# Last half's norms moved from GpSimd to VectorE, with new orders for the last pieces of a four-stage kernel

## What is computed

```python
# attention layer (six of them), per batch of 1024 rows
h1 = _ln(h + sa, l1w, l1b)
h2 = _ln(h1, l2w, l2b)
ff = relu(h2 @ w1.T + b1) @ w2.T + b2
h  = _ln(h2 + ff, l3w, l3b)
# seam
x = x + h                      # then
x = x + _L1_ffn_ref(_layernorm(x))
# last block: every linear quantizes its input in blocks of 16
xq = fp4_quant_dequant(x)
h  = silu(xq @ wq_gate.T) * (xq @ wq_up.T)
y  = fp4_quant_dequant(h) @ wq_down.T
```

## Time and profile before

| what | value |
| --- | --- |
| median of 3 runs | 2740.74 us (2735.45 to 2745.2) |
| profiled execution, its own time | 2755.81 us |
| its span, first to last instruction | 2754.0 us |
| busy share TensorE / VectorE / ScalarE / GpSimd | 86% / 88% / 83% / 57% |
| mean granted TensorE clock | 0.948 of full speed |
| the last two row maxima of the attention | start 2619.03 us into the span |

### The profile page before, as it was taken

The page is one execution under the profiler, slowest core; times in us unless marked ns, Lnnn a source line. Parts: engine busy times, 40 slices in busy tenths (PEclk is TensorE's granted clock), DMA queues, the critical chain, the costliest instruction groups (busy, mean ns, idle before and its releaser), DMA issues.

```text
span 2754.0 us, 93639 instructions
## 1 busy us (share of the span) xinstructions
PE 2356.9 (86%) x38225; PEld 1248.3 (45%) x38225; DVE 2422.1 (88%) x3331; ACT 2297.2 (83%) x4208; POOL 1562.0 (57%) x2959
## 2 busy tenths in 40 slices
PE   5777576799999998999989998999999999899846
PEld 3444365344444444444444444444444444444435
DVE  4888744799999999999999999999999999999956
ACT  5888533599999999999999999999999999999832
POOL 4879764535664466544664456644665446643564
PEclk8888888799999999999999999999999999999977
DMA  3222223311101111011110111101010111100000
GB/s 95 78 92 73 69 77 84 90 48 51 45 29 39 49 47 43 25 48 42 54 36 32 48 35 57 35 37 48 31 54 31 48 43 37 35 33 11 2 1 16
DMA packets 52140, 127.22 MB, mean 46 GB/s; under 512 B 6017, under 2 KB 40705, under 8 KB 47233
## 3 DMA queue, kind: packets, MB, share of 16 engines
q1 hardware_dynamic: 43329, 113.12, 12.3%
q0 software_dynamic: 2432, 5.08, 0.6%
q10 hardware_dynamic: 5952, 3.04, 0.4%
HBM read 96.09 MB, written 29.18 MB: 45 GB/s over the span
## 4 chain that ended last, share of the span: by engine, by line
PE 35%; issue 19%; POOL 17%; DVE 12%; ACT 12%; DMA 1%; POOLq 0%; SPq 0%; ACTq 0%; DVEq 0%; another core or an unknown queue 0%
PE bank L708 11%; PE bank L777 11%; PE bank L788 9%; ACT E L1048 9%; DVE NM L1417 8%; POOL hC L1553 2%; POOL acc L1659 2%; POOL H L1669 1%; ACT acc L999 1%; POOL smp L1652 1%; POOL H L1672 1%; PE bank L689 1%; POOL hC L1556 1%; POOL dg L1717 1%; PE bank L702 1%
## 5 line engine op out<-in xcount | busy, mean ns | idle before, releaser
L1417 DVE TENSOR_REDUCE NM<-bank 128x1 f32<-128x1024 f32 x1536 | 1799.6, 1208 | 73.2 <-PE bank L777 52.5
L1048 ACT ACTIVATE E<-bank,NM 128x1024 f32<-128x1024 f32 x1536 | 1707.4, 1118 | 161.6 <-DVE NM L1417 135.8
L777 PE MATMUL bank<-KS,QS 72*32 72x512 bf16 x12288 | 957.3, 387 | 161.9 <-ACT E L1048 112.4
L788 PE MATMUL bank<-E,dg 128*32 128x256 f32 x12288 | 924.6, 385 | 1.7 <-ACT acc L999 1.7
L1717 POOL TENSOR_TENSOR dg<-mask,RZ 128x128 f32<-128x128 f32 x384 | 152.9, 398 | 823.9 <-DVE RZ L1427 728.1
L777 PEld LDWEIGHTS bank<-KS,QS 72*32 72x32 bf16 x12288 | 251.8, 96 | 706.9 <-ACT E L1048 592.6
L788 PEld LDWEIGHTS bank<-E,dg 128*32 128x32 f32 x12288 | 384.7, 111 | 290.2 <-issue 60.9
L1048 ACT ACTIVATION_READ_ACCUMULATOR E<-bank,NM 128x1 f32 x1536 | 310.7, 202 | 0.0
L1659 POOL TENSOR_TENSOR acc<-acc,rel 128x256 f32<-128x256 f32 x384 | 272.2, 729 | 7.8 <-ACT acc L999 7.8
L708 PE MATMUL bank<-H,ET 128*32 128x129 f32 x6144 | 189.3, 275 | 6.3 <-DVE ET L1360 6.3
L708 PE MATMUL bank<-hT,WL 128*32 128x256 f32 x2304 | 164.0, 388 | 26.3 <-ACT UB L1010 22.0
(11 more groups left out here) (261 smaller groups left out, 2679.4 us busy)
## 6 DMA issues: line engine op xcount, KB each, us to landing
QS<-scratch SPq DMA_DIRECT2D x69, 384.0 KB
KS<-scratch SPq DMA_DIRECT2D x22, 1152.0 KB
scratch<-UB SPq DMA_DIRECT2D x144, 128.0 KB
CB<-crows SPq DMA_DIRECT2D x32, 512.0 KB, 3.8
WL<-in_wl SPq DMA_DIRECT2D x6, 1091.0 KB, 21.4
KS<-scratch SPq DMA_DIRECT2D x6, 384.0 KB
first<-in_fill SPq DMA_DIRECT2D x8, 247.5 KB, 4.2
second<-in_fill SPq DMA_DIRECT2D x8, 247.5 KB, 4.1
```

Of the source, the lines that this page charges most:

```text
L777: inst = PE_.matmul(bank[x % 3][32 * i:32 * i + 32, k * 512:k * 512 + 512], QS[0:72, half % 2, 4 * hq + i, r0:r0 + 32], KS[0:72, b, k, 4 * ...
L788: inst = PE_.matmul(pb(6)[32 * k:32 * k + 32, 256 * grp:256 * grp + 256], dg[:, x // 4 % 3, x % 4, :], E[:, x % NE, :].rearrange("p (i k c ...
L1048: A_.activation(E[:, x % NE, :], bank[x % 3][:, :], ACT.Exp, bias=NM[:, x % 4:x % 4 + 1], accum_out=ZS[:, quad % 3, j:j + 1]).then_inc(s[" ...
L1417: V.tensor_reduce(NM[:, x % 4:x % 4 + 1], bank[x % 3][:, :], AX.X, ALU.max, negate=True).then_inc(s["rowmax"], 1)
```

## The change

The last half's three norms no longer use `pv` and `ln`. On VectorE `nv` aggregates the statistics (`bn_aggr`, one a tile) and adds epsilon; GpSimd's `pw` is now a single power; `na` computes (x - mean) * gain and `nb` that times the power plus the offset, each one combined instruction a row tile, four a norm. For the third norm `nb` adds into `X`, so `fin` goes as a piece of its own, and GpSimd adds the offset to `X` beforehand (`xb`). The second norm's result goes to the `H` buffer. `h2t` may start tile by tile. `END_DUE` and `LAST` have new orders, and a table `NEAR_DUE` for half 22 puts its third norm later. No work of the attention steps is touched.

```diff
-            "POOL": {(7, "f"): "pv0", (8, "f"): "pw0", (9, "f"): "ln00 ln01 ln02 ln03 ln04 ln05 ln06",
...
+           "DVE": {(7, "e"): "nv0 na0 nb0", (8, "m"): "bn10 bn11 bn12 bn13 nv1 na1 nb1",
+                (11, "m"): "add2 bn20 bn21 bn22 bn23 nv2 na2", (12, "m"): "nb2"},
+           "POOL": {(7, "f"): "pw0", (8, "f"): "pw1", (11, "d"): "hb0 hb1", (11, "f"): "xb", (13, "f"): "pw2"}}
...
+        def end_norm_dve(e, own, n, p):
+            a, k = n % 2, int(p[2])
+            var = smp[:, a, k, :, :]
+            src, dst = (ZA[:, a], ZA[:, a], HB)[k], (ZA[:, a], next_h(n), HB)[k]
+            gain, offset = (wl(n // 4, "ln", 256 * k + 128 * i, 128) for i in range(2))
+            if p[:2] == "nv":
+                if k == 0:
+                    e.wait_ge(s["tbn0"], 4 * n + 4)
+                    own.count(V.scalar_tensor_tensor(var[:, :, 3], ZW[:, a, :, 128], EPS / 4.0, ZW[:, a, :, 128], ALU.mult, ALU.mult))
+                else:
+                    e.wait_ge(s["tbn"], 8 * n + 5 * k - 1)
+                for t in range(4):
+                    own.count(V.bn_aggr(var[:, t, 0:2], st[:, a, k, t, :]))
+                e.wait_ge(own.sem, own.n)
+                if k == 0:
+                    V.tensor_tensor(var[:, :, 2], var[:, :, 1], var[:, :, 3], ALU.add).then_inc(s["tbn0"], 1)
+                else:
+                    V.tensor_scalar(var[:, :, 2], var[:, :, 1], EPS, None, ALU.add).then_inc(s["tbn"], 1)
+            elif p[:2] == "na":
+                for t in range(4):
+                    own.count(V.scalar_tensor_tensor(dst[:, t, :], src[:, t, :], var[:, t, 0:1], gain, ALU.subtract, ALU.mult))
+            else:
+                e.wait_ge(own.sem, own.n)
+                e.wait_ge(s["tpow"], 3 * n + k + 1)
+                for t in range(4):
+                    r = n // 2 % 2 * 8 + 4 * (n % 2) + t
+                    out, more = (X[:, r, :], X[:, r, :]) if k == 2 else (dst[:, t, :], offset)
+                    inst = V.scalar_tensor_tensor(out, dst[:, t, :], var[:, t, 3:4], more, ALU.mult, ALU.add)
...
+            elif p[:2] == "pw" and n == HALF_N - 1:
...
+                G.tensor_tensor(smp[:, a, k, :, 3], smp[:, a, k, :, 2], mhalf[:, 0:4], ALU.pow).then_inc(s["tpow"], 1)
+            elif p == "xb":
+                r0 = b * 8 + 4 * hf
+                G.tensor_tensor(X[:, r0:r0 + 4, :], X[:, r0:r0 + 4, :],
+                                wl(l, "ln", 640, 128).unsqueeze(1).to_broadcast([128, 4, 128]), ALU.add)
```

More of the change, by code:

```diff
@@ L179 @@
                 (46, "d"): "sp08 sp09", (46, "f"): "sp10 sp11 sp12 sp13", (47, "d"): "sp14 sp15"}}
-END_DUE = {"PE": {(17, "h"): "h2t", (18, "h"): "ff1_00 ff1_01", (19, "g"): "ff1_10 ff1_11",
[14 rows of a table removed]
-STEPS = PAIRS + 71
-LAST = {"PE": {(1, "g"): "wt", (10, "g"): "tq0", (13, "g"): "gu0", (16, "g"): "gu1", (18, "h"): "tq1", (19, "h"): "ht0",
[5 rows of a table removed]
+NEAR_DUE = {engine: dict(at) for engine, at in HALF_DUE.items()}
+NEAR_DUE["DVE"] = {(11, "m"): "bn10 bn11", (11, "e"): "bn12 bn13", (29, "e"): "add2", (38, "m"): "bn20 bn21 bn22 bn23"}
+NEAR_DUE["POOL"] = {at: HALF_DUE["POOL"][at] for at in HALF_DUE["POOL"] if at[0] < 35}
+NEAR_DUE["POOL"].update({(37, "f"): "pv2", (38, "d"): "pw2", (38, "f"): "ln20 ln21 ln22 ln23", (42, "d"): "ln24 ln25 ln26 ln27 fin"})
+END_DUE = {"PE": {(8, "g"): "h2t", (8, "h"): "ff1_00 ff1_01", (9, "h"): "ff1_10 ff1_11",
[6 rows of a table added]
+STEPS = PAIRS + 71
+LAST = {"PE": {(3, "g"): "wt", (6, "g"): "tq0", (7, "g"): "gu0", (8, "g"): "tq1", (9, "g"): "gu1", (12, "g"): "ht0 gu2", (13, "g"): "dn0 ht1 dn1",
[3 rows of a table added]
         "DVE": {(-14, "m"): "wq00", (-14, "e"): "wq01", (-13, "m"): "wq02", (-13, "e"): "wq03", (-12, "m"): "wq04",
@@ L254, in due @@
     for half in range(max(-2, step // 32 - 3), min(HALF_N, step // 32 + 1)):
-        places = END_DUE if half == HALF_N - 1 else HALF_DUE
+        places = END_DUE if half == HALF_N - 1 else NEAR_DUE if half == HALF_N - 2 else HALF_DUE
         for p in places[engine].get((step - 32 * half - 31 - (8 if half == -2 else 0), place), "").split():
@@ L728, in post_pe @@
             elif p == "h2t":
-                e.wait_ge(s["tln"], 12 * n + 8)
+                src = HB[:, :, :] if n < HALF_N - 1 else next_h(n)
+                if n < HALF_N - 1:
+                    e.wait_ge(s["tln"], 12 * n + 8)
                 for t in range(4):
-                    inst = PE_.transpose(o[:, t * 128:t * 128 + 128], HB[:, t, :], ident[:, :])
+                    if n == HALF_N - 1:
+                        e.wait_ge(s["add1"], TILES + t + 1)
+                    inst = PE_.transpose(o[:, t * 128:t * 128 + 128], src[:, t, :], ident[:, :])
                 inst.then_inc(s["h2t"], 1)
@@ L1185, in scan_dve @@
                 for n, x in PROJECT["DVE"].get(p, ()):
-                    post_dve(e, n, x)
+                    post_dve(e, own, n, x)
                 if p in KNOWN["DVE"]:
@@ L1345, in unit_dve, with post_dve @@
                     V.scalar_tensor_tensor(x[:, 0:128], pb(n % 2)[:, 0:128], 0.5, x[:, 0:128], ALU.mult, ALU.add).then_inc(s["unit_out"], 1)
-        def post_dve(e, n, p):
+        def end_norm_dve(e, own, n, p):
[26 more added lines that the diff above has]
+                    inst = V.scalar_tensor_tensor(out, dst[:, t, :], var[:, t, 3:4], more, ALU.mult, ALU.add)
+                    if k == 0:
+                        own.count(inst)
+                    elif k == 1:
+                        inst.then_inc(s["add1"], 1)
+                    elif t == 3:
+                        inst.then_inc(s["fin"], 1)
+        def post_dve(e, own, n, p):
+            if p[:2] in ("nv", "na", "nb"):
+                end_norm_dve(e, own, n, p)
+                return
             if p in ("part1", "part3"):
@@ L1378, in post_dve @@
                 if k == 1:
-                    e.wait_ge(s["tln"], 12 * n + 1 + t)
+                    if n < HALF_N - 1:
+                        e.wait_ge(s["tln"], 12 * n + 1 + t)
+                    else:
+                        e.wait_ge(own.sem, own.n)
                 elif t == 0:
@@ L1428, in attention_dve @@
                 for n, p in due("DVE", q, "m"):
-                    post_dve(e, n, p)
+                    post_dve(e, own, n, p)
                 for j, p in second("DVE", q, "m"):
@@ L1647, in post_pool @@
                     G.tensor_tensor(y[:, :, 0], y[:, :, 0], y[:, :, 3], ALU.add).then_inc(s["tvar"], 1)
+            elif p[:2] == "pw" and n == HALF_N - 1:
+                k = int(p[2])
+                if k == 0:
+                    e.wait_ge(s["tbn0"], 4 * n + 5)
+                else:
+                    e.wait_ge(s["tbn"], 8 * n + 5 * k)
+                G.tensor_tensor(smp[:, a, k, :, 3], smp[:, a, k, :, 2], mhalf[:, 0:4], ALU.pow).then_inc(s["tpow"], 1)
[3 more added lines that the diff above has]
+                                wl(l, "ln", 640, 128).unsqueeze(1).to_broadcast([128, 4, 128]), ALU.add)
             elif p[:2] == "pw":
@@ L1677, in post_pool @@
                 h = int(p[2])
-                e.wait_ge(s["tln"], 12 * n + 6 + 2 * h)
-                G.tensor_tensor(ZA[:, a, 2 * h:2 * h + 2, :], HB[:, 2 * h:2 * h + 2, :],
+                if n < HALF_N - 1:
+                    e.wait_ge(s["tln"], 12 * n + 6 + 2 * h)
+                else:
+                    e.wait_ge(s["add1"], TILES + 2 + 2 * h)
+                h2 = HB[:, :, :] if n < HALF_N - 1 else next_h(n)
+                G.tensor_tensor(ZA[:, a, 2 * h:2 * h + 2, :], h2[:, 2 * h:2 * h + 2, :],
                                 wl(l, "ln", 768, 128).unsqueeze(1).to_broadcast([128, 2, 128]), ALU.add).then_inc(s["h2b"], 2)
```

## The result

| | before | changed |
| --- | --- | --- |
| median, first measurement (4 runs each) | 2740.20 us | 2722.95 us (2722.21 to 2733.77) |
| ratio | 1 | 0.9947, 95% interval 0.9932 to 0.9961 |
| median, second measurement (21 and 6 runs) | 2738.44 us | 2726.85 us (2722.72 to 2731.10) |
| ratio | 1 | 0.9960, 95% interval 0.9948 to 0.9973 |
| span of the profiled execution | 2754.0 us | 2731.9 us |

The kernel is faster: 14.5 us by the first ratio, 11.0 by the second. The forecast was 2722, range 2711 to 2733, 19 us less. The time lies within the range, but the gain is smaller than forecast, and one has to look at the parts to see by how much.

A forecast was written before the change was run, and what follows sets the result against it. The attention is bound by its own queues and unchanged; the tail is VectorE's work and waits. Start 2630.7 + work 86.3 + waits 8.2 + end 9.85 = 2735.1 against 2754.0, 19 us less: 2722 us, range 2711 to 2733.

The forecast's parts named there:

- The start: Start of VectorE's own tail: half 22's third norm moved behind the last `rel`, so `turn` starts 3.5 us earlier, at 2630.0.
- VectorE's work: VectorE's busy time in the tail: 78.7 us before, 89.3 with the norms, less 3.0 for less GpSimd interference, 86.3.
- VectorE's waits: VectorE's idle time in the tail: 27.0 us before, 8.2 after (2.6 before `sw0`, 5.6 in the loop).
- To the second norm's result: Last half's path to the second norm's result: 2643.7 against 2664.16, the largest step, 20 us earlier.
- The sum of the feed-forward: Start of `add2` in the last half: at 2664 us against 2692.31 before.
- the rival of the feed-forward's chain: `h2t` to `add2` takes 28 us again instead of 20, so the end comes later: 2733 us, chance 0.12.
- The end: Requantization, transposes, down projection and store behind `qh7`: 9.85 us, left alone by the change.
- three marks of being wrong: `add2` after 2672, combined instructions over 1.5 us a group of four, or waits for silu staying at 12.
- the low clock: Rival: TensorE stays at the low clock in the tail, about 10 us on `ff2` and four `gu`: 2732, chance 0.13.
- `pw2` ahead of `rh0` freezes the quantization: Slower rival: `pw2` on GpSimd holds every quantization behind pair 0; 2753 us if `add2` comes at 2695; chance 0.03.
- The covered loop: Rival: VectorE waits only 2.6 us in the tail and loses nothing to GpSimd: 27 us less, 2714, chance 0.12.
- The table load: ScalarE's load behind the first relu: 1.28 us, next activation 0.02 behind it, no drain; by the skill's page 2.66.

The follow-up runs named there:

- near_undone: The changed kernel with half 22's third norm back at its old places, ahead of the last half's first power; ratio to before 0.9970, tail 119.05 us.
- nb2_psum: The changed kernel with the third norm's four combined instructions taking their second tensor from PSUM, sum with `X` left out; ratio to before 0.9938, tail 112.68 us.
- rh0_ahead_rh1_behind: The changed kernel with `rh0` ahead of the third norm's power on GpSimd and `rh1` behind `pr3`; ratio to before 0.9941, tail 112.67 us.
- gu_ahead_both: rh0_ahead_rh1_behind with gate-up 6 and 7 ahead of `ht4` and `ht5`, and gate-up 1 ahead of the second group's transposes; ratio to before 0.9958, tail 109.46 us.

## Why the prediction was right in direction and too large in size

Its sum, on the tail's clock: the forecast's end at 2735.1 is 110.4 us behind the last but one `turn` (2624.69); measured 116.9 and 115.9, 5.5 to 6.5 more. The terms:

- *The start*, 3.5 us: the last `turn` came 3.94 earlier (8.86 to 4.92). The size is right, its parts are not: near_undone puts half 22's norm at 5.1 where the prediction had 3.15, and without it the last `turn` comes 1.1 later than before.
- *VectorE's work*, 86.3. In the first profile, from the end of the last `turn`, 2620.62, to the end of `qh7`, 2722.10, there are 101.5 us, of which the bracketed waits make 9.5 (0.72, 0.18, 3.41, 0.77, 0.18, 3.62, 0.66): 91.9 of work. **This is the term that was mis-sized**, by 5.6 (91.8 in the second profile). The six groups of combined instructions were put at 1.13 each, 6.8; they took 2.08 + 2.94 + 1.13 + 1.77 + 1.13 + 6.28 = 15.3, 8.5 more. Something else went the other way: all other instructions together lost 12.6 us against their shortest times before and 7.8 now, 4.8 less, where the prediction took 3.0 off. The prediction named the rule that says so, from the Trainium skill's page "SBUF — State Buffer", section "Who interferes with whom", held the trace to agree, and then gave it 2 us for norms 0 and 1 alone, outside the sum. These two lost 3.4 us, and the third norm, which it left out, 5.2. For the combined instructions the runs bear the rule out: with both tensors in SBUF each is held for about one GpSimd instruction, and with one of them in PSUM it is not. But the two durations that the prediction gave for it, 1.48 and 0.53, are those of a `TENSOR_SCALAR` with one input. They show the same wait, and no need of two inputs. What I missed is in my own order rows: `rh0` and `rh1` stand behind `pw2` on GpSimd and `nb2` waits for `pw2`, so both start at the same moment. One instruction of VectorE is let through for each one of GpSimd, and here the small one paid each time. I had asked of `pw2` only whom it makes wait, and not beside what those then run.
- *VectorE's waits*, 8.2: measured 9.5. The sum was nearly right, its parts were not. `sw0`, put at 2.6, did not wait (1.3 in the second profile; `qt1` took 6.1 instead of 4.3, again beside GpSimd's large pieces); silu 1 cost 4.2 that I had not listed; the loop cost 4.3 for 5.6. The 7.9, 4.3 and 3.1 us of waits that I let go are gone. That the sum of this term came out near is in part luck.
- *To the second norm's result*, 20 us earlier: 39.47 became 21.70, 17.8 earlier, just under the 18 that I had named. The slowed groups, 3.4 us, are more than the rest.
- *The sum of the feed-forward* at 39.3: came at 44.9 and 43.4, below the 47 that I had set as the mark of being wrong. From the first transpose to the sum it took 24.4 and 22.9 us, where the prediction gave 20 and the kernel before took 28.2; so the rival of the feed-forward's chain came in part. `ff2` ran at the full clock (granted 1.00), 128 instructions in 3.70.
- *The end*, 9.85: 9.80.

Of my three marks of being wrong, one was met: the combined instructions took over 1.5 us a group of four, in four groups of six. The sum did not come after its mark, and the waits for silu fell from 11.7 to 8.5. So the path and the waits that I gave up were right, and the price of the work that moved was not.

Of the rivals, the low clock was at most a small part of the miss: gate-up 0 and 1 took 3.69 and 4.01 and the later ones 2.5 to 3.7, and `ff2` ran at the full clock. Between the two profiles of the changed kernel, gate-up 1 at 4.01 and at 2.63 goes with 1.0 us at the end. That `pw2` ahead of `rh0` freezes the quantization did happen as a mechanism, with GpSimd idle for 15.8 us, and its price was not the wait but the collision after it: the tail of nb2_psum, where `pw2` still stands ahead, is as short as that of rh0_ahead_rh1_behind, where it does not hold back `rh0`. The covered loop did not come. The table load cost what the row said, 1.28 and 0.01 behind it.

The median of the first measurement met the forecast to 1 us. That is luck: it is 17 below the median of before, and the tail and the second measurement give 11 to 13. A gain of 12.4 lies under the 15 to 24 that I had given 0.60, between the low clock's 9 and the forecast, where the prediction has no rival of its own.

## What to carry to other kernels

When work moves from GpSimd to VectorE, look at what GpSimd does at that moment: a combined instruction with two inputs in SBUF took 0.28 us beside nothing and 1.5 to 1.8 beside GpSimd's large pieces, and a one-input `TENSOR_SCALAR` 1.22 instead of 0.18. If a wait releases both engines at once, as `pw2` did in both profiles of the changed kernel, they collide; move GpSimd's large pieces away from that moment, or take one operand from PSUM, and look at what the moved pieces then lie beside. Here that was worth 3.2 us with both pieces moved and 0.7 with one. And an order and the length of the pieces in it are one decision: here the new order alone lost 6.7 us, and on top of short norms it gained 5.5 to 6.5.

## What the runs showed of the hardware

- VectorE beside GpSimd: four 128x128 combined instructions took 1.13, 3.67 and 6.28 us beside none, two and four GpSimd instructions of 1.4 to 1.7 us, and 1.12 inside a single one of 1.66 us when one of their tensors lay in PSUM. Beside GpSimd's power of four numbers (1.04 us) they took 1.13, as alone. One-input `TENSOR_SCALAR` instructions are held too (1.22 for 0.18).
- GpSimd is held less: its pieces beside the 6.28 us kept their length, but beside `qt2` in rh0_ahead_rh1_behind one took 1.71 us instead of 1.39.
- The time ahead of the attention differs between executions and between chips: the first row maximum lay at 496.6 and 489.7 us in two profiles of the changed kernel, and in the profiles known to be of one chip at 489.7 to 495.0, in those of the other at 506.8 to 510.8. The tail repeated to 1 us in two profiles of the changed kernel. For a change in a tail, the stretch in the profile tells more than the whole span, but gu_ahead_both shows that one profile does not stand for all runs.
